# One DRAM sum for the layer-1 experts' results, with weights copied early, paired w_down loads and deeper prefetch

## The chip, the core and the metric

One core of a Trainium2 chip runs the whole program. The metric is the device time of one execution in microseconds. Lower is better.

## The reference, cut to what matters

Two transformer layers over 2048 tokens of 512 numbers. The part that the change touches:

```python
# layer 1 attention, keys: a small feature network with a bias fb1, applied to every head of k
#   feature = act(k_head @ fw1 + fb1) ...
# layer 1 feed-forward: 64 experts, 6 per token
topk_w, topk_ids = grouped_topk(sigmoid(x @ gate_w), bias)       # E = 64, K = 6, 8 groups, 4 kept
h   = silu(buf[e] @ w_gate[e]) * (buf[e] @ w_up[e])             # H = 512, F = 192
out = h @ w_down[e]                                             # F = 192 -> 512
y   = segment_sum(out[...] * topk_w, token)                     # each token: sum over its 6 experts
x   = layernorm(x + shared(x) + y)
```

## The kernel before

Matrix products are made in three passes (`mm3`, L64 to L68): both operands are split in a high and a low part, and high x high, high x low and low x high are added in PSUM. So every weight is copied to its high part by ACT and subtracted to its low part by DVE. Engines run programs of their own and meet at semaphores.

**Keys of layer 1** (`attention1_keys`). 16 tiles of 128 tokens. For each tile TensorE computes values (12 matmuls of 512 columns), then features: four groups of `mm3` with 128 rows of contraction and 256 columns (L66 to L68), each followed by one matmul that adds the bias from two rows (`ones2`, `fb_hl`, L1417), then sums (L1391, L1393) and the next keys.

**Shared expert and routing** (`experts1_shared`). Makes the tables `token_of` and `target_of` (which tokens an expert takes, and where its results go), and starts two DRAM sums: `sums[0]` with the residual, `sums[1]` with zeros (L1977, four DMAs of 1 MB out of a tile that DVE uses again at L2230), and spare rows of zeros.

**Routed experts** (`experts1_routed`). 64 experts of at most 96 tokens each. `three_stages` (L488) writes out each engine's order of work. Step g does on every engine, in this order: `ahead` for item g+3, `first` for g+1, `between` for g-1, `prepare` for g+1, `second` for g, `third` for g-1; the middle of the loop is a hardware loop unrolled U = 4 times. What an expert e passes through:

- SP loads (L2352, L2356): w_down of e when the low part of w_down of e-4 has been made, gate/up weights of e likewise. Four raw buffers of each.
- POOL `gather` (L2363 to L2372): copies the index (L2368), then an indirect DMA (L2371) brings 96 rows of 512 features and 64 expert shares into `xg`. It waits for the results of expert e-4, since `results` (L2472) still reads its scale from `xg`. Four buffers.
- PE `turn` (L2398), ACT and DVE parts (L2440, L2487), weight parts (L2447, L2482), gate/up products, silu (L2465), hidden (L2498), w_down parts (L2461, L2500), hidden turned (L2418), `down` with 96 rows of contraction twice.
- ACT `results` (L2472): scales by the share and writes `y`. Four buffers.
- POOL `add_results` (L2374 to L2383): copies the target (L2378), and an indirect DMA with add (L2382) adds 96 rows of 2 KB to `sums[e % 2]`. Two experts can hold the same token, so an add may only be issued when the last one to the same sum has landed: with two sums, that of e-2.

POOL's order in step g is gather(g+3), then add(g-1).

**Combine** (`combine1`). 8 groups of 256 rows: load both sums (L2520, L2521), add them on DVE (L2539), statistics (L93, L95), `rstd` on POOL (L100, L102), apply (L106), store (L2524).

Of the kernel before, what the change touches and what calls it, by code (L numbers as in the profile page):

```python
# [28 lines left out]
P = 128  # L29
# [458 lines left out]
def three_stages(eng, n, first, second, third, ahead=no_work, between=no_work, prepare=no_work, unroll=2):  # L488
# [5 lines left out]
    def step(g):  # L494

        for stage, item in ((ahead, g + 3), (first, g + 1), (between, g - 1), (prepare, g + 1), (second, g), (third, g - 1)):
            if 0 <= item < n:
                stage(item // unroll, item % unroll)


    rounds = (n - 4) // unroll
    for g in range(-3, unroll + 1):
        step(g)
    with eng.Fori(1, rounds) as i:
        for q in range(unroll):
            at = lambda stage, item: stage(i + item // unroll, item % unroll)
            at(ahead, q + 4)
# [694 lines left out]
def attention1_keys(k, xt, w):  # L1202
# [5 lines left out]
    with ExitStack() as ctx:  # L1208
# [7 lines left out]
        fb1 = sb("fb1", [2, FM])  # L1216
        part = sb("part", [2, 1])
        rest = sb("rest", [2, 1])
        fb_hi, fb_lo = sb("fb_hi", [2, FM], F32R), sb("fb_lo", [2, FM])
        fb_hl = sb("fb_hl", [2, 4, FM], F32R)  # L1220
        ones_f, ones2 = sb("ones_f", [2, P]), sb("ones2", [2, P], F32R)
# [63 lines left out]
        with nc.Block() as block:  # L1285
            @block.sync
            def _(sp):
# [5 lines left out]
                sp.dma_start(fb1[:, :], io["fb1"].partition_broadcast(2)).then_inc(s_fb, 16)  # L1293
# [3 lines left out]
                sp.wait_ge(s_zero, 12)  # L1297
# [11 lines left out]
            def _(pool):  # L1309
# [10 lines left out]
                pool.memset(rest[:, :], 1.0).then_inc(s_zero, 1)  # L1320
# [5 lines left out]
                pool.memset(part[0:1, :], 1.0).then_inc(s_zero, 1)  # L1326
                pool.memset(rest[0:1, :], 0.0).then_inc(s_zero, 1)
# [143 lines left out]
            def _(vec):  # L1471
# [4 lines left out]
                def feature_weights():  # L1476
                    vec.wait_ge(s_fw, 64)
                    vec.wait_ge(s_zero, 10)
# [408 lines left out]
def experts1_shared(k):  # L1887
# [6 lines left out]
    k.s_sums0, k.s_sums1 = k.sem("e1_first_sums_begun"), k.sem("e1_second_sums_begun")  # L1894
    k.w1_first = rt("w1_first", [P, KD, 2 * F1])
    k.s_w1_first = k.sem("e1_gate_up_loaded0")
    with ExitStack() as ctx:
# [66 lines left out]
        with nc.Block() as block:  # L1964
            @block.sync
            def _(sp):
# [17 lines left out]
                for c in range(NC):  # L1984
                    sp.wait_ge(s_res, TC * (c + 1))
                    sp.dma_start(k.sums[0][0:T, :].rearrange("(c j p) d -> c p j d", p=P, j=TC)[c],
                                 k.x[:, c * TC:(c + 1) * TC, :]).then_inc(k.s_sums0, 16)
# [183 lines left out]
            def _(vec):  # L2171
# [13 lines left out]
                def choose():  # L2185
# [42 lines left out]
                    vec.wait_ge(k.s_sums1, 16 * (NC + 2))  # L2228
# [82 lines left out]
def experts1_routed(k):  # L2311

    nc, bank, io = k.nc, k.bank, k.io
    with ExitStack() as ctx:
        U = 4
        two = lambda name, shape, dt=F32: [k.sb(f"e1_{name}{p}", shape, dt, ctx) for p in range(2)] * 2
        four = lambda name, shape, dt=F32: [k.sb(f"e1_{name}{p}", shape, dt, ctx) for p in range(U)]
        w1_raw = [k.w1_first] + [k.sb(f"e1_w1_raw{p}", [P, KD, 2 * F1], F32, ctx) for p in range(1, U)]
        w1_hi, w1_lo = two("w1_hi", [P, KD, 2 * F1], F32R), two("w1_lo", [P, KD, 2 * F1], F32R)
        w2_raw, w2_hi, w2_lo = four("w2_raw", [HF1, 2, D]), two("w2_hi", [HF1, 2, D], F32R), two("w2_lo", [HF1, 2, D], F32R)  # L2320
# [4 lines left out]
        si, hf = two("si", [CAP, F1]), two("hf", [CAP, F1])  # L2325
        ht_hi, ht_lo = two("ht_hi", [HF1, 2 * CAP], F32R), two("ht_lo", [HF1, 2 * CAP], F32R)
        y = four("y", [CAP, D])

        each = lambda name: [k.sem(f"e1_{name}{p}") for p in range(U)]
        sem = lambda n: k.sem("e1_" + n)  # L2330
        s_w = [k.s_w1_first] + [sem(f"gate_up_loaded{p}") for p in range(1, U)]
        s_v, s_g = each("down_loaded"), each("rows_gathered")
        s_y = [sem(f"results_added{a}") for a in range(2)]
# [8 lines left out]
        added = lambda h, p: 16 * (U // 2 * h + p // 2)  # L2342

        with nc.Block() as block:
            @block.sync
            def _(sp):
                def load(h, p):
# [14 lines left out]
            def _(pool):  # L2362
                def gather(h, p):  # L2363
# [10 lines left out]
                def add_results(h, p):  # L2374
                    e = U * h + p
                    if past(h, p, 2):
                        pool.wait_ge(s_y[p % 2], added(h, p))
# [4 lines left out]
                    pool.indirect_dma_start(k.sums[p % 2], bass.IndirectOffsetOnAxis(target[p][:, 0:1], 0), y[p][:, :], None,  # L2382
                                            compute_op=ALU.add).then_inc(s_y[p % 2], 16)  # L2383

                pool.wait_ge(k.s_sums0, 16 * NC)
                pool.wait_ge(k.s_sums1, 16 * (NC + 2))
                three_stages(pool, E1, nothing, nothing, add_results, ahead=gather, unroll=U)
                for a in range(2):
                    pool.wait_ge(s_y[a], 16 * E1 // 2)
# [231 lines left out]
```

## Time and profile before

| | us |
|---|---|
| median of 3 runs (1843.55 to 1856.09) | 1854.52 |
| the profiled execution | 1854.76 |
| its span in the trace | 1853.0 |

The profiled execution lies 0.2 us above the median, and 1.8 us of it lie outside of the span. Matmuls are pipelined and their ends modelled, so the distance from one start to the next tells more than a busy time. "q1 hardware_dynamic" are the DMAs that SP issues (weights among them), "q0 software_dynamic" those of POOL (gathers and adds).

### The profile page before, as it was taken

To read this page: it belongs to the slowest core of one execution; us is meant where nothing else is said; L and a number is where in the kernel's file an instruction comes from. 1 tells how busy PE (TensorE), PEld (TensorE's weight loads), DVE (VectorE), ACT (ScalarE), POOL (GpSimd) and SP (SyncE) were. 2 spreads that over 40 slices of the span, in tenths; PEclk is the share of its full clock that TensorE was granted. 3 is DMA by queue.
4 is the path that set the end of the run, shared out by engine and by line. 5 is a ranking of instruction groups with operands and counts; after the bars stand their busy time and mean duration, and the time that the engine had idled before them with its cause. 6 is when DMAs were issued, how large, how long until landed. Compare 5 with 4: busy or idle time off the path is not lost. (4 is left out here: it accounts for less than half of the span.)

```text
span 1853.0 us, 24141 instructions
## 1 busy us (share of the span) xinstructions
PE 1491.7 (81%) x8165; PEld 1249.9 (67%) x8166; DVE 1112.4 (60%) x1841; ACT 721.8 (39%) x1127; POOL 643.8 (35%) x738
## 2 busy tenths in 40 slices
PE   6999699997999996399997999688767767777760
PEld 5787476766999996388886888465555545555550
DVE  5787572345676774586535666366855555555556
ACT  3211230004666663144444444132135555555550
POOL 1455300003222221355331433115425554555553
PEclk8999899998999999699987999697768898888895
DMA  3000300007888884321000000231177888877767
GB/s 143 1 1 29 110 24 1 1 0 241 281 283 283 279 280 160 94 65 39 12 1 29 1 24 23 75 117 57 46 216 232 232 236 229 239 220 228 220 139 272
DMA packets 114934, 239.15 MB, mean 129 GB/s; under 512 B 13853, under 2 KB 48669, under 8 KB 114863
## 3 DMA queue, kind: packets, MB, share of 16 engines
q1 hardware_dynamic: 87647, 170.57, 27.8%
q0 software_dynamic: 18784, 51.39, 11.0%
q10 hardware_dynamic: 8432, 16.25, 2.3%
q8 instruction: 43, 0.70, 0.2%
q14 instruction: 28, 0.23, 0.0%
HBM read 187.45 MB, written 50.72 MB: 129 GB/s over the span
## 5 line engine op out<-in xcount | busy, mean ns | idle before, releaser
L66 PE MATMUL bank<-e_xt_hi,e_w_hi 128*128 128x256 f32 x496 | 142.9, 288 | 0.0
L2398 PE MATMUL bank<-ident,e_xg 96*128 96x96 f32 x256 | 40.1, 287 | 127.3 <-DMA e_xg<-rows,e_index 127.1
L68 PE MATMUL bank<-e_xt_hi,e_w_lo 128*128 128x256 f32 x496 | 140.2, 283 | 0.0
L67 PE MATMUL bank<-e_xt_lo,e_w_hi 128*128 128x256 f32 x496 | 140.1, 282 | 0.0
L2382 POOL DMA_INDIRECT sums<-e_y,e_target x64 | 117.9, 1842 | 58.5 <-POOL e_target L2378 22.1
L1047 POOL COPY e_index<-r_token_of 128x2 int32 (+1 forms) x31 | 7.9, 254 | 370.1 <-POOLq L602 203.4
L2398 PEld LDWEIGHTS bank<-ident,e_xg 96*128 96x128 f32 x256 | 28.1, 159 | 152.2 <-DMA e_xg<-rows,e_index 80.0
L1148 DVE TENSOR_TENSOR e_w_lo<-e_raw,e_w_hi 128x2048 fp32r<-128x2048 f32 x31 | 71.0, 2292 | 85.3 <-ACT e_w_hi L1105 70.8
L2487 DVE TENSOR_TENSOR e_xt_lo<-bank,e_xt_hi 128x384 fp32r<-128x384 f32 x64 | 35.6, 557 | 130.5 <-ACT e_xt_hi L2440 117.7
L66 PE MATMUL bank<-e_w_hi,e_xt_hi 128*96 128x384 f32 x256 | 106.4, 416 | 1.7 <-DVE e_w_lo L2482 1.7
L2482 DVE TENSOR_TENSOR e_w_lo<-e_w_raw,e_w_hi 128x1536 fp32r<-128x1536 f32 x48 | 84.4, 1759 | 35.5 <-ACT e_w_hi L2447 33.2
L68 PE MATMUL bank<-e_w_hi,e_xt_lo 128*96 128x384 f32 x256 | 102.3, 399 | 0.0
L67 PE MATMUL bank<-e_w_lo,e_xt_hi 128*96 128x384 f32 x256 | 102.0, 398 | 0.0
L67 PEld LDWEIGHTS bank<-e_xt_lo,e_w_hi 128*128 128x128 f32 x496 | 94.2, 190 | 0.0
L66 PEld LDWEIGHTS bank<-e_xt_hi,e_w_hi 128*128 128x128 f32 x496 | 94.1, 190 | 0.0
L68 PEld LDWEIGHTS bank<-e_xt_hi,e_w_lo 128*128 128x128 f32 x496 | 94.0, 189 | 0.0
L231 POOL TENSOR_TENSOR a_read<-a_read_n 128x256 f32<-128x256 f32 x64 | 50.2, 785 | 103.3 <-DVE a_read_n L452 103.3
L2440 ACT ACTIVATE e_xt_hi<-bank 128x384 fp32r<-128x384 f32 x64 | 31.2, 487 | 138.1 <-PE bank L2398 138.0
L1651 POOL TENSOR_TENSOR q_g_lo<-q_gf,q_g_hi 128x512 fp32r<-128x512 f32 x32 | 41.6, 1299 | 111.8 <-ACT q_g_hi L1765 111.8
L66 PE MATMUL bank<-s_xt_hi,s_w_hi 128*128 128x512 f32 (+1 forms) x192 | 78.6, 410 | 0.8 <-ACT s_scores L2148 0.8
L2371 POOL DMA_INDIRECT e_xg<-rows,e_index x64 | 61.1, 955 | 52.2 <-POOL e_index L2368 50.2
L1105 ACT ACTIVATE e_w_hi<-e_raw 128x2048 fp32r<-128x2048 f32 x31 | 59.4, 1916 | 49.2 <-DMA e_raw<-in_rw 29.4
(452 smaller groups left out, 5050.4 us busy)
## 6 DMA issues: line engine op xcount, KB each, us to landing
e_w_raw<-in_w_gate_up SPq DMA_DIRECT2D x48, 768.0 KB, 5.8
e_raw<-in_rw SPq DMA_DIRECT2D x62, 512.0 KB
e_w_raw<-in_w_down SPq DMA_DIRECT2D x64, 384.0 KB
e_raw<-in_rg SPq DMA_DIRECT2D x31, 512.0 KB
results<-e_y ACTq DMA_DIRECT2D x31, 512.0 KB, 5.7
r_w_first<-in_w_gate_up SPq DMA_DIRECT2D x16, 768.0 KB, 7.0
rows<-resid SPq DMA_DIRECT2D x8, 1024.0 KB, 4.3
resid<-in_x SPq DMA_DIRECT2D x4, 1024.0 KB, 11.3
```

Source lines behind the costliest of these rows:

```text
L66: pe.matmul(out, a_hi, b_hi, start=start, stop=False)
L67: pe.matmul(out, a_hi, b_lo, start=False, stop=False)
L68: return pe.matmul(out, a_lo, b_hi, start=False, stop=stop)
L231: pool.tensor_tensor(read_2[:, v % 2, :], read_n[:, v % 2, 0:256], read_n[:, v % 2, 256:512], ALU.add).then_inc(s_r2, 1)
L1105: act.activation(w_hi[p][:, 0:2 * W], raw[p][:, 0:2 * W], ACT.Copy).then_inc(s_whi, 1)
L1148: vec.tensor_tensor(w_lo[p][:, 0:2 * W], raw[p][:, 0:2 * W], w_hi[p][:, 0:2 * W], ALU.subtract).then_inc(s_wlo, 1)
L1651: pool.tensor_tensor(g_lo[:, c % 2, f], gf[:, u % 2, :], g_hi[:, c % 2, f].bitcast(F32), ALU.subtract).then_inc(s_glo, 1)
L2371: pool.indirect_dma_start(xg[p][:, :], None, k.rows1, bass.IndirectOffsetOnAxis(index[p][:, 0:1], 0)).then_inc(s_g[p], 16)
L2382: pool.indirect_dma_start(k.sums[p % 2], bass.IndirectOffsetOnAxis(target[p][:, 0:1], 0), y[p][:, :], None, compute_op=ALU.add).then_inc(s ...
L2398: mm = pe.transpose(bank[p % 2][:, b * CAP:(b + 1) * CAP], xg[p][:, b * P:(b + 1) * P], k.ident[0:CAP, 0:CAP])
L2482: vec.tensor_tensor(w1_lo[p][:, :, :], w1_raw[p][:, :, :], w1_hi[p][:, :, :], ALU.subtract).then_inc(s_wlo, 1)
L2487: vec.tensor_tensor(xt_lo[p][:, :], bank[p % 2][:, 0:KD * CAP], xt_hi[p][:, :], ALU.subtract).then_inc(s_tlo, 1)
```

## The change

1. **One sum.** `k.sums` is one DRAM tensor. add(e) waits for add(e-1) to land, not add(e-2). Four stores of 1 MB of zeros and one of spare rows go. `combine1` loads one sum, and DVE's add goes.
2. **Weights copied early.** DVE copies the expert's share out of `xg` into `weight` (96 x 1) right after `turned_lo`; gather(e) now waits for the copy of e-4 (`s_wt`), not for its results.
3. **Paired w_down loads.** w_down of two experts (3 x 128 rows) comes in one DMA of 128 partitions x 6 KB per two experts, not two of 96 x 4 KB. An even expert's parts are made of two blocks (1024 numbers per partition), an odd one's of one (512). The hidden tile is padded with zeros to 2 x 128 columns, so that `down` contracts 128 rows twice; each expert's 192 rows lie in blocks (0, 1) or (1, 2).
4. **Deeper prefetch.** U = 8, eight raw gate/up buffers and four raw pairs; `lead=6` on SP: loads run six experts ahead. All other engines keep `lead=3`, and gathers, targets and `y` keep four buffers (NX).
5. **Keys.** The bias operands `fb1`, `part`, `rest`, `ones_f`, `ones2`, `fb_hl` of `attention1_keys` have 128 partitions instead of 2, all but the first two rows zero in effect (`rest`, `part`), so the bias matmul contracts 128 rows. One more memset and one more wait on POOL.

```diff
-        for stage, item in ((ahead, g + 3), (first, g + 1), ...
+        for stage, item in ((ahead, g + lead), (first, g + 1), ...
@@ attention1_keys
-        fb1 = sb("fb1", [2, FM])
+        fb1 = sb("fb1", [P, FM])
...
-        ones_f, ones2 = sb("ones_f", [2, P]), sb("ones2", [2, P], F32R)
+        ones_f, ones2 = sb("ones_f", [P, P]), sb("ones2", [P, P], F32R)
@@ experts1_shared, SP
                 sp.wait_ge(s_zeros, 1)
-                for c in range(NC):
-                    sp.dma_start(k.sums[1][0:T, :].rearrange("(c j p) d -> c p j d", p=P, j=TC)[c],
-                                 zeros.unsqueeze(1).to_broadcast([P, TC, D])).then_inc(k.s_sums1, 16)
-                sp.dma_start(k.sums[0][T:T + CAP, :], zeros[0:CAP]).then_inc(k.s_sums1, 16)
-                sp.dma_start(k.sums[1][T:T + CAP, :], zeros[0:CAP]).then_inc(k.s_sums1, 16)
+                sp.dma_start(k.sums[T:T + CAP, :], zeros[0:CAP]).then_inc(k.s_spare, 16)
@@ experts1_routed, SP
-                    if past(h, p, U):
-                        sp.wait_ge(s_vlo, e - U + 1)
-                    sp.dma_start(w2_raw[p][:, :, :].rearrange("p f n -> p (f n)"),
-                                 io["w_down"][bass.ds(e, 1)].rearrange("e p n -> p (e n)")).then_inc(s_v[p], 16)
-                three_stages(sp, E1, nothing, nothing, nothing, ahead=load, unroll=U)
+                    if p % 2 == 0:
+                        if past(h, p, U):
+                            sp.wait_ge(s_vlo, e - U + 2)
+                        sp.dma_start(w2_raw[p][:, :, :].rearrange("p f n -> p (f n)"),
+                                     io["w_down"][bass.ds(U // 2 * h + p // 2, 1)].rearrange("q p n -> p (q n)")).then_inc(s_v[p], 16)
+                three_stages(sp, E1, nothing, nothing, nothing, ahead=load, unroll=U, lead=6)
@@ POOL
                 def gather(h, p):
-                    if past(h, p, U):
-                        pool.wait_ge(s_g[p], 16 * h)
-                        pool.wait_ge(s_ysb, e - U + 1)
+                    if past(h, p, NX):
+                        pool.wait_ge(s_g[p], gathered(h, p) - 16)
+                        pool.wait_ge(s_wt, e - NX + 1)
...
                 def add_results(h, p):
-                    if past(h, p, 2):
-                        pool.wait_ge(s_y[p % 2], added(h, p))
+                    if past(h, p, 1):
+                        pool.wait_ge(s_y, 16 * e)
...
-                    pool.indirect_dma_start(k.sums[p % 2], ...
+                    pool.indirect_dma_start(k.sums, ...
@@ PE, ACT, DVE
-                        mm = mm3(pe, bank[6 + p % 2][0:CAP, :], ht_hi[p][:, c], ht_lo[p][:, c], w2_hi[p][:, f, :], w2_lo[p][:, f, :],
+                        mm = mm3(pe, bank[6 + p % 2][0:CAP, :], ht_hi[p][:, c], ht_lo[p][:, c], w2_hi[p][:, p % 2 + f, :], w2_lo[p][:, p % 2 + f, :],
...
-                    if past(h, p, U):
-                        act.wait_ge(s_y[p % 2], added(h, p) - 16)
+                    if past(h, p, NX):
+                        act.wait_ge(s_y, 16 * (e - NX + 1))
+                    act.wait_ge(s_wt, e + 1)
...
+                    if past(h, p, NX):
+                        vec.wait_ge(s_ysb, e - NX + 1)
+                    vec.tensor_copy(weight[p][:, :], xg[p][:, bass.ds(D + e, 1)]).then_inc(s_wt, 1)
@@ combine1
-                    sp.dma_start(k.x[:, c * NL:(c + 1) * NL, :], tiles(k.sums[0][0:T, :])[c]).then_inc(s_a[c], 16)
-                    sp.dma_start(other[:, c * NL:(c + 1) * NL, :], tiles(k.sums[1][0:T, :])[c]).then_inc(s_b[c], 16)
+                    sp.dma_start(k.x[:, c * NL:(c + 1) * NL, :], tiles(k.sums[0:T, :])[c]).then_inc(s_a[c], 16)
...
-                    vec.tensor_tensor(k.x[:, t, :], k.x[:, t, :], other[:, t, :], ALU.add).then_inc(s_sum, 1)
```

## Rows read from the trace of the kernel before

**Rows 1.** The page's first line.
```profile
span 1853.0 us, 24141 instructions
```
**Rows 2.** Windows: stretch, us, each engine busy (instructions), TensorE clock, DMA share, GB/s.
```profile
786.00:966.00 180.00, 177.49 (x1036) 151.47 (x1034) 111.97 (x160) 77.97 (x148) 82.27 (x72) 0.93 0.10 30
1352.00:1380.00 28.00, 14.81 (x68) 11.72 (x68) 12.88 (x16) 12.84 (x18) 7.54 (x11) 0.65 0.86 274
1380.00:1802.00 422.00, 303.11 (x1468) 241.86 (x1468) 243.15 (x305) 239.59 (x366) 227.13 (x245) 0.86 0.78 222
1813.00:1853.00 40.00, 0.00 (x0) 0.00 (x0) 29.54 (x56) 0.00 (x0) 16.68 (x16) 0.50 0.84 315
...
799.00:813.00 14.00, 14.00 (x86) 11.90 (x85) 12.70 (x20) 6.84 (x14) 8.36 (x8) 1.00 0.18 53
```
**Rows 3.** Tile `e_target`: the adds, minimum/median/maximum ns, first and last start.
```profile
L2382 POOL DMA_INDIRECT sums<-e_y,e_target x64: 1422/1830/3022, 1380.3 to 1801.9; - x64
```
**Rows 4.** Timeline around one turn of the loop's chain: start, us, what, idle before.
```profile
1560.50 0.68 ACT L2472 ACTIVATE e_y<-bank,e_xg 96x512 f32<-96x512 f32 x1 [1.38 <-PE bank L68]
...
1562.39 0.95 POOL L2371 DMA_INDIRECT e_xg<-rows,e_index  x1 [0.80 <-POOL e_index L2368]
...
1569.56 0.55 PE L2398 MATMUL bank<-ident,e_xg 96*128 96x96 f32 x4 [1.50 <-DMA e_xg<-rows,e_index]
...
1573.89 0.68 ACT L2472 ACTIVATE e_y<-bank,e_xg 96x512 f32<-96x512 f32 x1 [0.50 <-PE bank L68]
```
**Rows 5.** Tile `e_xg` in 1400:1780: gathers, from issue to landing.
```profile
DMA to landing us min/median/max: 4.1/4.9/7.4
```
**Rows 6.** Timeline of TensorE in the keys stage, features of one tile.
```profile
909.44 0.28 PE L67 MATMUL bank<-a_fw_lo,k_k_hi 128*128 128x256 f32 x1
909.56 0.28 PE L68 MATMUL bank<-a_fw_hi,k_k_lo 128*128 128x256 f32 x1
909.77 0.38 PE L1417 MATMUL bank<-k_fb_hl,k_ones 2*128 2x256 f32 x1
910.08 0.39 PE L66 MATMUL bank<-a_fw_hi,k_k_hi 128*128 128x256 f32 x1
910.30 0.28 PE L67 MATMUL bank<-a_fw_lo,k_k_hi 128*128 128x256 f32 x1
```
**Rows 7.** Groups of TensorE in 786:970: the bias matmul.
```profile
L1417 PE MATMUL bank<-k_fb_hl,k_ones 2*128 2x256 f32 x64 | 24.4, 381 | 0.0
```
**Rows 8.** Timeline of POOL: adds and target copies.
```profile
1511.55 1.84 POOL L2382 DMA_INDIRECT sums<-e_y,e_target  x1 [0.85 <-ACT e_y L2472]
...
1571.06 0.20 POOL L2378 COPY e_target<-r_target_of 96x1 int32 x1
...
1572.12 1.45 POOL L2382 DMA_INDIRECT sums<-e_y,e_target  x1 [0.86 <-POOL e_target L2378]
...
1788.47 1.84 POOL L2382 DMA_INDIRECT sums<-e_y,e_target  x1 [0.85 <-ACT e_y L2472]
...
1793.05 0.18 POOL L2378 COPY e_target<-r_target_of 96x1 int32<-96x1 int32 x1 [0.24 <-DMA sums<-e_y,e_target]
```
**Rows 9.** DMA queues in 1512.6:1516.7, 1516.7:1519, 1574.1:1576.1, 1576.1:1579.5, 1405:1780: packets, MB, share of 16 engines.
```profile
q1 hardware_dynamic: 225, 1.09, 86.7%
...
q0 software_dynamic: 175, 0.42, 72.9%
...
q0 software_dynamic: 118, 0.20, 79.5%
...
q1 hardware_dynamic: 205, 0.96, 85.7%
...
q1 hardware_dynamic: 13854, 63.83, 51.4%
```
**Rows 10.** Timeline of DVE in the combine: first additions, statistics and apply.
```profile
1818.06 1.22 DVE L2539 TENSOR_TENSOR resid<-resid,c_other 128x1024 f32<-128x1024 f32 x1 [19.34 <-DMA c_other<-sums]
...
1821.76 1.22 DVE L2539 TENSOR_TENSOR resid<-resid,c_other 128x1024 f32<-128x1024 f32 x1 [0.74 <-DMA c_other<-sums]
...
1824.64 0.97 DVE L106 TENSOR_SCALAR resid<-resid,mv,rstd 128x512 f32<-128x512 f32 x2
1825.53 1.22 DVE L2539 TENSOR_TENSOR resid<-resid,c_other 128x1024 f32<-128x1024 f32 x1
```

More of the change, by code:

```diff
@@ L485, in no_work, with three_stages @@
     pass
-def three_stages(eng, n, first, second, third, ahead=no_work, between=no_work, prepare=no_work, unroll=2):
+def three_stages(eng, n, first, second, third, ahead=no_work, between=no_work, prepare=no_work, unroll=2, lead=3):
     def step(g):
-        for stage, item in ((ahead, g + 3), (first, g + 1), (between, g - 1), (prepare, g + 1), (second, g), (third, g - 1)):
+        for stage, item in ((ahead, g + lead), (first, g + 1), (between, g - 1), (prepare, g + 1), (second, g), (third, g - 1)):
             if 0 <= item < n:
                 stage(item // unroll, item % unroll)
-    rounds = (n - 4) // unroll
-    for g in range(-3, unroll + 1):
+    rounds = (n - lead - 1) // unroll
+    for g in range(-lead, unroll + 1):
         step(g)
@@ L2324, in experts1_routed @@
         xt_hi, xt_lo = two("xt_hi", [P, KD * CAP], F32R), two("xt_lo", [P, KD * CAP], F32R)
-        si, hf = two("si", [CAP, F1]), two("hf", [CAP, F1])
-        ht_hi, ht_lo = two("ht_hi", [HF1, 2 * CAP], F32R), two("ht_lo", [HF1, 2 * CAP], F32R)
+        weight = four("weight", [CAP, 1])
+        si, hf = two("si", [CAP, F1]), two("hf", [CAP, 2 * P])
+        own = lambda p: slice(p % 2 * (2 * P - F1), p % 2 * (2 * P - F1) + F1)
+        other = lambda p: slice(F1, 2 * P) if p % 2 == 0 else slice(0, 2 * P - F1)
+        ht_hi, ht_lo = two("ht_hi", [P, 2 * CAP], F32R), two("ht_lo", [P, 2 * CAP], F32R)
         y = four("y", [CAP, D])
-        each = lambda name: [k.sem(f"e1_{name}{p}") for p in range(U)]
         sem = lambda n: k.sem("e1_" + n)
         s_w = [k.s_w1_first] + [sem(f"gate_up_loaded{p}") for p in range(1, U)]
-        s_v, s_g = each("down_loaded"), each("rows_gathered")
-        s_y = [sem(f"results_added{a}") for a in range(2)]
+        s_v = [a for a in [k.sem(f"e1_down_loaded{q}") for q in range(U // 2)] for _ in range(2)]
+        s_g = [k.sem(f"e1_rows_gathered{p}") for p in range(NX)] * (U // NX)
+        s_zero, s_wt = sem("hidden_zeroed"), sem("weights_kept")
+        gathered = lambda h, p: 16 * (U // NX * h + p // NX + 1)
+        s_y = sem("results_added")
         s_ix, s_go, s_to = sem("index"), sem("index_seen"), sem("target")
@@ L2381, in add_results @@
                     pool.sem_inc(s_go, 1)
[L2382 to L2386, printed above, removed]
+                    pool.indirect_dma_start(k.sums, bass.IndirectOffsetOnAxis(target[p][:, 0:1], 0), y[p][:, :], None,
+                                            compute_op=ALU.add).then_inc(s_y, 16)
+                pool.wait_ge(k.s_sums, 16 * NC)
+                pool.wait_ge(k.s_spare, 16)
                 three_stages(pool, E1, nothing, nothing, add_results, ahead=gather, unroll=U)
-                for a in range(2):
-                    pool.wait_ge(s_y[a], 16 * E1 // 2)
+                pool.wait_ge(s_y, 16 * E1)
             @block.tensor
@@ L2393, in turn @@
                 def turn(h, p):
[L2394 removed]
+                    pe.wait_ge(s_g[p], gathered(h, p))
                     if past(h, p, 2):
@@ L2453, in hidden_hi @@
                         act.wait_ge(s_dn, e - 1)
-                    act.activation(ht_hi[p][:, :], bank[4 + p % 2][0:HF1, 0:2 * CAP], ACT.Copy).then_inc(s_hh, 1)
+                    act.activation(ht_hi[p][:, :], bank[4 + p % 2][:, 0:2 * CAP], ACT.Copy).then_inc(s_hh, 1)
                 def silu(h, p):
@@ L2510, in combine1 @@
     with ExitStack() as ctx:
-        other = k.sb("c1_other", [P, NT, D], F32, ctx)
-        s_a, s_b = ([k.sem(f"c1_{n}_loaded{c}") for c in range(NG)] for n in ("first", "second"))
-        s_sum = k.sem("c1_summed")
+        s_a = [k.sem(f"c1_sums_loaded{c}") for c in range(NG)]
         s_stat, s_var, s_rstd, s_ln, s_st = (k.sem("c1_" + n) for n in ("stats", "var", "rstd", "normed", "stored"))
@@ L2562, in two_layers @@
         k.rows1 = nc.dram_tensor("rows1", (T, D + E1), F32, kind="Internal").ap()
-        k.sums = [nc.dram_tensor(f"sums{a}", (T + CAP, D), F32, kind="Internal").ap() for a in range(2)]
+        k.sums = nc.dram_tensor("sums", (T + CAP, D), F32, kind="Internal").ap()
         setup(k)
```

65 lines of the change are left out of this document (34 added, 31 removed).

## The prediction

> **What bounds the kernel now.** I read the windows by stage first, then the stretches that the change touches. The profiled execution took 1854.8 us, 0.2 over the median, so the sum is made against 1854.8 [rows 1].
>
> In the keys stage TensorE is busy for 177.5 of 180 us: it alone sets the pace there, at a granted clock of 0.93 of full speed [rows 2]. Inside the features the full-height matmuls of 256 columns start 0.12 us apart, but around a bias matmul of two rows the spacing is 0.21 before it, 0.31 after its start, and 0.22 after the next start. One group of four takes 909.44 to 910.30, 0.86 us [rows 6].
>
> In the routed loop no engine is full: of 422 us TensorE is busy 303, DVE 243, ACT 240, POOL 227, and the DMA engines have a share of 0.78 [rows 2]. The 64 adds run from 1380.3 to 1801.9, so an expert takes 421.6 / 63 = 6.69 us [rows 3]. One turn of what holds it: results written at 1560.50, the gather that they release is issued at 1562.39, TensorE turns its rows at 1569.56, having waited for that DMA, and 4.3 us later, at 1573.89, results are written again [rows 4]. That is two steps in 13.4 us. The gather needs 4.1 to 7.4 us, 4.9 in the middle [rows 5]. So the loop is bound by the gather's latency, since `results` still reads `xg`. The steps themselves take 4.3 us.
>
> The combine, 1813 to 1853, is DVE's: after a first wait it repeats add, statistics, apply in 1825.53 - 1821.76 = 3.77 us [rows 2, 10].
>
> **The change part by part.**
>
> *Keys.* With 128 rows the bias matmul has the shape of its neighbours, which start 0.12 us apart, so a group of four should take 4 x 0.12 = 0.48 and not 0.86 us: 0.38 x 64 groups [rows 7] = 24.4 us less, all on the engine that sets the pace. The clock's mean of 0.93 means (1 - 0.93) x 180 = 12.6 us lost to half-speed stretches [rows 2]. They come while TensorE is never idle, so I suspect the sparse features, and put a third of it down as won: 4 us (bounds 0 and 12.6). DVE becomes the next limit in the first tiles: 12.7 of 14 us busy [rows 2] is 0.91 of a tile that is to shrink by 14%. For some six tiles that costs back about 0.5 us each, 3 us at most; I take 1. Sum: -28 (bounds -18 and -36). The wider memsets, the DMA of `fb1` to 128 partitions and one more POOL wait lie beside the loading of the stage and are costed at nothing; uncovered, they are below 1 us together.
>
> The Trainium skill (TensorE: Matmul & The Clock Gate, section LDWEIGHTS) says that loading 32 rows takes the same time as loading 128, as only columns count. By that alone the height of the bias operand would be worth nothing and the sum 28 us higher; the row speaks against it, as the neighbours with the same columns keep 0.12 us and this one does not [rows 6].
>
> *Combine.* Eight additions of 1.22 us go, 7 of them in rounds of DVE that start right behind one another and the first in front: 8 x 1.17 (the starts overlap by 0.05) = 9.4 us [rows 10]. Half of the loads go, so DVE starts on 0.5 MB instead of 1 MB, at 315 GB/s and more [rows 2] some 1.2 us earlier, and the 0.74 us wait for the second pair goes too, less what of it the shorter first round uncovers. Sum: -10.9 (bounds -9 and -12). Late next is still DVE, 2.6 us a group.
>
> *The stores of zeros.* Some 4.6 MB less written while TensorE and DVE set the pace of routing, and DVE never waited for them: 0.
>
> *The gather.* It no longer waits for the results of e-4 but for a copy made a step and more earlier. In POOL's order it stands behind add(g-2), so it leaves when that add has been issued. From there: add 1.8, index copy and issue some 2.0, gather 4.9 to 7.4, step 4.3, results to add 1.1 = 14 to 17 us for three steps: 4.7 to 5.5 us each. The gather's latency stops being the bound. DMA needs 0.78 x 6.69 = 5.2 us of all engines per expert [rows 2, 3], unchanged in bytes. ACT and DVE get about 0.3 us shorter (a quarter less of w_down on average) and DVE a copy of one column longer; neither was the bound.
>
> *The single sum.* This is what is late next. add(e) now goes out only when add(e-1) has landed. The period is: issue to release, then the target copy 0.20, then 0.86 to the issue [rows 8]. Queued behind this wait on POOL is the next gather, and behind that the whole loop. How long is issue to release? Low end: the add of 1788.47 freed the copy at 1793.05 after 4.58 us, when no weights were loaded any more [rows 8]; period 4.58 + 0.2 + 0.86 = 5.6 us. In mid-loop the add of 1572.12 had all its packets done by 1576.1, after which queue q0 has none [rows 8, 9]. High end: the add of 1511.55 had no packet moved until 1516.7, while q1 moved 1.09 MB of weights, and ended before 1519, 7.4 us after its issue [rows 8, 9]; with 0.6 to the release (4.58 against the 4.0 of the add of 1572.12) and 1.06 to the next issue the period is 9.1. Weights hold 51% of the DMA engines' time [rows 9], and the deeper prefetch bundles them: SP waits once per two experts for w_down's low part and then issues a pair and two gate/up loads, 2.3 MB. One of two adds should fall into such a bundle: (5.6 + 9.1) / 2 = 7.35. Against it, a gather now leaves some 4 us before the add and not 2, so the two no longer share the queue. I take 7.0 us (bounds 5.6 and 9.1). The last seven adds see no weights, since these run eight ahead: 5.6. Sum: 56 x 7.0 + 7 x 5.6 = 431 against 421.6, +9.6 us. The start, 1352 to 1380, is bound by gathers under a full queue and stays.
>
> Together: 1854.8 - 28 - 10.9 + 0 + 9.6 = 1825.5; I say 1825.
>
> **The rivals.**
>
> *Adds land fast.* If the adds fall mostly between the bundles, or get their turn among the weights, the period is 5.6 to 6.2. With 5.9: 56 x 5.9 + 39 = 370, -52 us, and 1854.8 - 28 - 10.9 - 52 = 1764; the floor, all at 5.6, is 1747. For it: the mid-loop add that took 4.0 us. Against it: the add of 1511.55, and that DMA would then be busy 5.2 of 5.9 us, with ever fewer gaps.
>
> The Trainium skill (DMA: Bandwidth & Descriptors, section Anatomy of one DMA) gives for a DMA of this path 2.0 us plus bytes / 436e3, an estimate of 2.5 us for 197 KB. By that page the chain of adds would not bind at all and this rival would win; the rows show 4.0 at the least.
>
> *The chain of adds costs more than all else gives (the other side).* Place: POOL's wait before L2378. Price: the keys and the combine give 38.9 us, so the kernel gets no faster if 56 x P + 39 = 460.5, P = 7.5 us; it is 1% slower from P = 7.9 on. With P = 8.0: 487, +66, 1882 us. For it: two adds of three would have to meet a bundle like that of 1511.55, and 2.3 MB at 274 GB/s [rows 2] last 8.4 us, more than one period. Against it: today's adds meet weights too, half of the time, and the loop holds 6.69.
>
> *The bias matmul's gap stays.* If it comes from something other than its two rows (its place, its bank), the keys give nothing: 1825 + 28 = 1853. Against it: the same shape without the gap stands beside it.
>
> **How the numbers follow.** Forecast (P from 6.5 to 7.5, keys as said): 1797 to 1853, chance 0.50. Fast adds: 0.22. Slow adds (P over 7.5): 0.18. Gap stays: 0.10. The range leaves out the faster half of the fast adds and the slower half of the slow ones: 1775 to 1872. A change of 1%, 18.5 us, is about what a measurement of this kernel can tell from none. Faster by over 1% (below 1836): 0.22 + 0.38 of the forecast's 0.50 = 0.60. Slower by over 1% (above 1873): half of the slow adds and a little of the last rival, 0.12. Same: 0.28. The predicted time is the forecast's own.
>
> **What would show it.** In the profile after: L1417 with starts 0.12 us apart from its neighbours, the keys stage some 150 us long and its clock closer to 1.00; in the loop TensorE's wait for the gather small or gone, and POOL's target copy waiting for the DMA of `sums` in nearly every step, at a period near 7; in the combine rounds of 2.6 us. The prediction is wrong if the adds' period is off (each 0.3 us is 17 us), if TensorE in the keys runs into ACT's or DVE's wait and gives only half, or if the loads bundled eight deep slow the gathers beyond their new slack.

## The result, and the profile after

The kernel after takes 1879.66 us (median of 4 runs, 1874.77 to 1885.87) against 1853.68 us for the kernel before: a ratio of 1.0153 with the interval 1.0103 to 1.0202: **slower by about 26 us, 1.5%**, which is small but clear of the noise. The forecast was 1825 us, with a range from 1775 to 1872. Below, P is the time of an expert in the routed loop: the last add's start less the first's, divided by 63.

The page's first line, after:
```profile
span 1876.2 us, 23909 instructions
```
Windows by stage of the kernel after (columns as in [rows 2]): keys, routed loop, combine.
```profile
799.00:939.00 140.00, 138.05 (x989) 129.67 (x988) 101.90 (x143) 71.50 (x142) 79.13 (x69) 0.98 0.11 30
...
1346.00:1838.00 492.00, 314.90 (x1482) 255.84 (x1480) 233.58 (x370) 228.99 (x370) 218.76 (x245) 0.81 0.65 190
1838.00:1876.00 38.00, 0.00 (x0) 0.00 (x0) 19.63 (x48) 0.00 (x0) 10.79 (x17) 0.50 0.65 226
```
One window of the kernel before, for the same 989 matmuls of the keys:
```profile
799.00:968.00 169.00, 169.00 (x989) 144.63 (x987) 102.25 (x143) 74.18 (x142) 78.77 (x69) 0.93 0.08 24
```
The adds after, by their tile (to set beside [rows 3]):
```profile
L2390 POOL DMA_INDIRECT sums<-e_y,e_target x64: 1423/1454/3024, 1346.0 to 1837.5; - x64
```
These rows split the 23.2 us by which the span grew. The first add starts 34.3 us earlier (1346.0 against 1380.3). From first to last add are 491.5 us and not 421.6: +69.9. From the last add to the end are 38.7 us and not 51.1: -12.4. The sum is +23.2. **Everything outside the loop gained what it was meant to and a little more; the loop lost more than all of it.** P went from 6.69 to 491.5 / 63 = 7.80 us, and the loop's DMA share fell from 0.78 to 0.65: nothing there is full.

*The loop.* Waits of the kernel after in 1346:1838 (engine, what waits, for whom: us in total, times, longest):
```profile
POOL e_target L2386 <- DMA sums<-e_y,e_target: 170.7, 59, 6.2
...
PE bank L2405 <- DMA e_xg<-rows,e_index: 165.9, 34, 7.1
```
POOL waits in nearly every step for the add before. TensorE's wait for the gather has not gone either: in 1352:1800 it is 158.7 us, where it was 127.1 before. The timeline of POOL shows why, in one full turn of two experts:
```profile
1542.23 1.46 POOL L2390 DMA_INDIRECT sums<-e_y,e_target  x1 [0.86 <-POOL e_target L2386]
1543.21 0.68 POOL L2376 COPY e_index<-r_token_of 96x1 int32 x1
1544.69 0.96 POOL L2379 DMA_INDIRECT e_xg<-rows,e_index  x1 [0.80 <-POOL e_index L2376]
1546.64 1.14 POOL L2386 COPY e_target<-r_target_of 96x1 int32 x1 [0.98 <-DMA sums<-e_y,e_target]
1548.62 1.76 POOL L2390 DMA_INDIRECT sums<-e_y,e_target  x1 [0.85 <-POOL e_target L2386]
1549.90 0.68 POOL L2376 COPY e_index<-r_token_of 96x1 int32 x1
1551.38 0.96 POOL L2379 DMA_INDIRECT e_xg<-rows,e_index  x1 [0.80 <-POOL e_index L2376]
1557.43 0.18 POOL L2386 COPY e_target<-r_target_of 96x1 int32 x1 [5.09 <-DMA sums<-e_y,e_target]
1558.46 1.45 POOL L2390 DMA_INDIRECT sums<-e_y,e_target  x1 [0.85 <-POOL e_target L2386]
```
The add of 1542.23 frees the next target copy after 4.4 us, the add of 1548.62 only after 8.8. The intervals are 6.39 and 9.84 us, in turn. What comes between is SP's bundle of three loads, issued as soon as VectorE has made the low part of w_down, 0.6 us behind the start of the second add's issue:
```profile
1548.37 0.68 DVE L2513 TENSOR_TENSOR e_w_lo<-e_w_raw,e_w_hi 128x512 fp32r<-128x512 f32 x1
...
1549.22 0.33 SPq L2361 DMA_DIRECT2D e_w_raw<-in_w_down  x1
...
1549.75 0.92 SPq L2356 DMA_DIRECT2D e_w_raw<-in_w_gate_up  x2
```
And the DMA queues, in 1544.2:1546.2 (the first add's packets), 1549.2:1554 (weights only, the second add has none), and 1554:1557 (both):
```profile
q0 software_dynamic: 112, 0.20, 79.9%
...
q1 hardware_dynamic: 211, 1.20, 75.9%
...
q1 hardware_dynamic: 138, 0.75, 63.0%
q0 software_dynamic: 129, 0.28, 42.1%
```
The second add's first packet moves 5.46 us after the start of its issue, its last at 8.05 us; without weights beside it the first add has 2.03 and 3.92 us. The pattern repeats every two experts: VectorE ends the w_down subtraction, which frees SP, at the point of the step where the next add goes out. The add was not ready ahead of the loads, though: its issue took POOL 1.76 us, to 1550.38, and the loads were issued from 1549.22 to 1550.67. Of the first 56 adds 25 land within 5 us and 31 later, and the mean interval behind them is 6.12 and 9.54 us; (25 x 6.12 + 31 x 9.54) / 56 = 8.01. The last 7 intervals, without weights, are 6.10 on average. The gather stands right behind the add in POOL's order and in queue q0, so behind a late add it lands late too (tile `e_xg` in 1400:1780):
```profile
DMA to landing us min/median/max: 5.8/7.7/8.9
```
This line knows the landing of 24 of the gathers there only, the ones behind the adds at SP's bundles. By their packets most of the others end about 3 us after their issue, and the mean of all is 5.1 us (5.4 in the kernel before). The line of [rows 5] likewise rests on 14 gathers of 55.


*The keys.* Timeline of TensorE in the kernel after, one group of four:
```profile
922.59 0.29 PE L66 MATMUL bank<-a_fw_hi,k_k_hi 128*128 128x256 f32 x1
...
922.94 0.28 PE L1419 MATMUL bank<-k_fb_hl,k_ones 128*128 128x256 f32 x1
923.06 0.28 PE L66 MATMUL bank<-a_fw_hi,k_k_hi 128*128 128x256 f32 x1
```
923.06 - 922.59 = 0.47 us where [rows 6] had 0.86. The stage's granted clock is 0.98 where it was 0.93.

*The combine.* DVE's rounds there (statistics, aggregate, apply):
```profile
1857.97 0.97 DVE L106 TENSOR_SCALAR resid<-resid,mv,rstd 128x512 f32<-128x512 f32 x2
1858.86 0.69 DVE L93 BATCH_NORM_STATS2 stats<-resid 128x6 f32<-128x512 f32 x1
...
1861.36 0.69 DVE L93 BATCH_NORM_STATS2 stats<-resid 128x6 f32<-128x512 f32 x1
```
A round is 1861.36 - 1858.86 = 2.50 us, against 3.77 in [rows 10].

### The profile page after: what moved, and what is told of

It is laid out like the page before. It is cut to its first block and busy times, and to the rows that moved or that the text cites. A ratio compares the mean times of both kernels' runs of the same rounds, so it can differ in the third digit from the quotient of the medians.

```text
span 1876.2 us, 23909 instructions
## 1 busy us (share of the span) xinstructions
PE 1468.7 (78%) x8165; PEld 1245.8 (66%) x8166; DVE 1089.8 (58%) x1897; ACT 705.7 (38%) x1127; POOL 629.2 (34%) x741
## 5 line engine op out<-in xcount | busy, mean ns | idle before, releaser
L2405 PEld LDWEIGHTS bank<-ident,e_xg 96*128 96x128 f32 x256 | 32.0, 171 | 197.7 <-DMA e_xg<-rows,e_index 115.0
L2390 POOL DMA_INDIRECT sums<-e_y,e_target x64 | 109.3, 1708 | 63.7 <-POOL e_target L2386 50.1
L2492 DVE TENSOR_TENSOR e_w_lo<-e_w_raw,e_w_hi 128x1536 fp32r<-128x1536 f32 x56 | 98.5, 1760 | 39.4 <-ACT e_w_hi L2456 38.6
L66 PE MATMUL bank<-e_w_hi,e_xt_hi 128*96 128x384 f32 x256 | 110.8, 433 | 0.2 <-DVE e_w_lo L2492 0.2
L2386 POOL COPY e_target<-r_target_of 96x1 int32 (+1 forms) x64 | 32.7, 512 | 170.8 <-DMA sums<-e_y,e_target 170.7
L2379 POOL DMA_INDIRECT e_xg<-rows,e_index x64 | 69.3, 1082 | 51.8 <-POOL e_index L2376 51.8
L2456 ACT ACTIVATE e_w_hi<-e_w_raw 128x1536 fp32r<-128x1536 f32 x56 | 83.2, 1486 | 0.0
```

The costliest lines, as they stand in the source:

```text
L66: pe.matmul(out, a_hi, b_hi, start=start, stop=False)
L2379: pool.indirect_dma_start(xg[p][:, :], None, k.rows1, bass.IndirectOffsetOnAxis(index[p][:, 0:1], 0)).then_inc(s_g[p], 16)
L2390: pool.indirect_dma_start(k.sums, bass.IndirectOffsetOnAxis(target[p][:, 0:1], 0), y[p][:, :], None, compute_op=ALU.add).then_inc(s_y, 16)
L2405: mm = pe.transpose(bank[p % 2][:, b * CAP:(b + 1) * CAP], xg[p][:, b * P:(b + 1) * P], k.ident[0:CAP, 0:CAP])
L2456: act.activation(w1_hi[p][:, :, :], w1_raw[p][:, :, :], ACT.Copy).then_inc(s_whi, 1)
L2492: vec.tensor_tensor(w1_lo[p][:, :, :], w1_raw[p][:, :, :], w1_hi[p][:, :, :], ALU.subtract).then_inc(s_wlo, 1)
```

## The experiments

Theory T1 (**bundle**): one sum makes a chain, issue, landing, target copy, issue, and the chain is long because every second add waits behind a bundle of weights. Theory T2 (**chain alone**): the chain takes over 7.3 us under any loads. Theory T3 (**held copy**): VectorE draws out POOL's copy and issue within the chain. Medians were measured beside the kernel before on the same chip; since its own median moves between 1852.8 and 1856.2 from group to group, ratios count. P, landing and gap are of one profiled execution each, which lay up to 6.4 us off its median (e13), so differences of P of 0.1 us tell nothing. The runs of e6 and e8 lie further apart than others (1853 to 1869, 1851 to 1868). Landing is the time from the start of an add's issue to the end of its last packet, and gap the time from there to the next issue, both as means of the first 56 adds.

| kernel | sums | weight copies | w_down loads | median us | ratio to before | P us | landing | gap |
|---|---|---|---|---|---|---|---|---|
| before | 2 | late | single | 1853.7 | 1 | 6.69 | 5.9 | 1.1 |
| after | 1 | early | pair | 1879.7 | 1.015 | 7.80 | 6.0 | 2.0 |
| e3 keys only | 2 | late | single | 1828.5 | 0.985 | 6.75 | 5.7 | 1.3 |
| e6 keys, one sum | 1 | late | single | 1866.4 | 1.004 | 7.49 | 5.8 | 1.9 |
| e7 keys, early | 2 | early | single | 1779.4 | 0.961 | 5.89 | 6.2 | - |
| e8 keys, early, one sum | 1 | early | single | 1865.1 | 1.003 | 7.60 | 5.9 | 1.9 |
| e1 two sums | 2 | early | pair | 1774.6 | 0.955 | 6.02 | 6.4 | - |
| e9 two sums, spread | 2 | early | pair at odd | 1759.7 | 0.949 | 5.71 | 5.9 | - |
| e11 e9, copy first | 2 | early | pair at odd | 1762.2 | 0.948 | 5.78 | 5.9 | - |
| e2 spread | 1 | early | pair at odd | 1843.3 | 0.994 | 7.34 | 5.7 | 1.8 |
| e5 copy first | 1 | early | pair | 1844.6 | 0.995 | 7.27 | 6.1 | 1.4 |
| e10 both | 1 | early | pair at odd | 1832.4 | 0.985 | 7.06 | 5.8 | 1.5 |
| e4 light loads | 1 | early | hardly any | 1780.5 | 0.959 | 6.22 | 4.2 | 2.1 |
| e12 light, copy first | 1 | early | hardly any | 1757.1 | 0.943 | 5.88 | 4.2 | 1.7 |
| e13 small subtraction | 1 | early | pair | 1842.0 | 0.994 | 7.32 | 5.8 | 1.7 |
| e14 one input | 1 | early | pair | 1835.7 | 0.989 | 7.11 | 5.6 | 1.7 |

**e1, the sum taken back.**
```diff
-                    if past(h, p, 1):
-                        pool.wait_ge(s_y, 16 * e)
+                    if past(h, p, 2):
+                        pool.wait_ge(s_y[p % 2], added(h, p))
...
-                    pool.indirect_dma_start(k.sums, ...
+                    pool.indirect_dma_start(k.sums[p % 2], ...
```
(the stores of zeros and the combine are those of the kernel before.)

> The kernel after, with two sums again (even experts add into one, odd experts into the other; both are zeroed, and the combine adds the two). Early weight copies, paired w_down loads and the new keys stay. If it is the chain through one sum that made the loop 7.80 us per expert, the loop falls to 5.5 to 6.2 us (the gather or the gate/up work bounds it, as 6.69 us did with later weight copies), 63 x 1.6 to 2.3 = 100 to 145 us less, and the combine takes its 12 us back: 1745 to 1790. If the paired loads themselves hold up the gathers, it gives back less: 6.7 us per expert and about 1820. The rival that neither is so (the loop is bound by loads at 200 GB/s) says 7.8 and about 1890.

Measured: 1774.61 us, ratio 0.9546 (0.9515 to 0.9576). The adds of this kernel:
```profile
L2395 POOL DMA_INDIRECT sums<-e_y,e_target x64: 1423/1455/2944, 1346.4 to 1725.5; - x64
```
379.1 / 63 = 6.02 us. **The one sum alone costs 105 us of time and turns a gain of 4.5% into a loss of 1.5%.** The adds land no sooner here (6.4 us on average, as the bundle hits them too); they only no longer follow one another.

**e2, the bundle spread.**
```diff
-                    if p % 2 == 0:
+                    if p % 2 == 1:
                         if past(h, p, U):
-                            sp.wait_ge(s_vlo, e - U + 2)
+                            sp.wait_ge(s_vlo, e - U + 1)
```


> The kernel after, but the paired w_down load is issued at the odd expert and not together with two gate/up loads, so that no single issue round puts more than the pair and one gate/up load on the queues. Bundle theory (every second add lands 8.0 us after its issue and not 3.9, since 1.5 to 2.2 MB of weights stand ahead of it): the late add gains 1 to 2 us, the period falls from 7.80 to about 7.2, 1830 to 1850. Chain theory (issue, landing, copy, issue take their time whatever the loads, and the bytes per two experts are the same): 7.7 to 7.9 us and 1870 to 1885.

Measured: 1843.29, ratio 0.9936 (0.9910 to 0.9962), P = 7.34. The late adds land after 7.1 us on average and not 7.65, the early ones unchanged at 3.9, and 31 of 56 are late, as in the kernel after. This is near T1's 7.2 and below T2's 7.7 to 7.9, but the bundle's form is worth 0.46 us and no more: the bytes still come. What refutes T2 is e4 below.

**e3, the keys alone** (the kernel before with `attention1_keys` of the kernel after).

> The kernel before with the keys of the kernel after alone (bias matmul moved). The first add came 34.3 us earlier in the kernel after, of which the keys show 29. If all 34 are the keys' own: 1819; if 5 belong to the early weight copies or the zeroing of one sum: about 1824; if the forecast's 24 were the matmuls alone and the clock gave nothing: 1830. The loop should stay at 6.69 us per expert.

Measured: 1828.51, ratio 0.9852 (0.9830 to 0.9873), 27.5 us less; P as before. Its windows:
```profile
799.00:940.00 141.00, 136.59 (x982) 128.41 (x980) 101.25 (x142) 71.47 (x141) 80.47 (x71) 0.98 0.10 28
1350.00:1774.00 424.00, 303.17 (x1468) 243.26 (x1468) 242.49 (x304) 239.84 (x366) 228.13 (x244) 0.86 0.78 220
```
The forecast had 28. From the first to the last bias matmul it is 143.5 us against 173.2. The start of the first add is no fine measure: in kernels whose code up to the loop is that of the kernel after it lay between 1340.4 and 1349.4.

**e4, the weights taken out.**
```diff
-                        sp.dma_start(w1_raw[p][:, :, :].rearrange(...), io["w_gate_up"][bass.ds(e, 1)]...)
+                        if past(h, p, U):
+                            sp.dma_start(w1_raw[p][:, 0, 0:16], io["w_gate_up"][0][:, 0:16]).then_inc(s_w[p], 16)
```
(and the same for w_down.)

> The kernel after, but from expert 8 on each weight load brings 16 columns of a block only (it leaves out nearly all of loading the weights of experts 8 to 63, which compute with stale ones). One sum stays. Bundle theory: no add meets weights, all land about 3.9 us after issue, and the period is that plus the copy and the issue, 5.6 to 6.6 us: 63 x 1.2 to 2.2 less than 1880, 1740 to 1800. Chain theory: adds are bound by their own 128 descriptors, the copies and VectorE beside them, and the period stays above 7.3: over 1845. The last seven adds of the kernel after, without weights beside them, took 5.3 and 6.6 us in turn, which speaks for about 6.

Measured: 1780.49, P = 6.22, landing 4.2 us. (An add is 112 packets of q0, as above, and not 128.) POOL's timeline there:
```profile
1541.10 1.45 POOL L2396 DMA_INDIRECT sums<-e_y,e_target  x1 [0.86 <-POOL e_target L2392]
...
1545.44 0.18 POOL L2392 COPY e_target<-r_target_of 96x1 int32 x1 [0.91 <-DMA sums<-e_y,e_target]
1546.47 2.12 POOL L2396 DMA_INDIRECT sums<-e_y,e_target  x1 [0.86 <-POOL e_target L2392]
...
1551.52 0.18 POOL L2392 COPY e_target<-r_target_of 96x1 int32 x1 [0.32 <-DMA sums<-e_y,e_target]
```
The alternation is gone: 53 of 56 adds land within 5 us. **7.80 - 6.22 = 1.58 us of P are the weights' doing**, and T2, which asked for over 7.3 under any loads, is refuted. But 6.22 us with hardly any loads is still more than the 6.02 of e1, which moves them all.

**e5, the target copy ahead of the wait.**
```diff
-                    if past(h, p, 1):
-                        pool.wait_ge(s_y, 16 * e)
                     pool.tensor_copy(target[p][:, :], k.target_of[:, bass.ds(e, 1)]).then_inc(s_to, 1)
                     pool.wait_ge(s_to, e + 1)
+                    if past(h, p, 1):
+                        pool.wait_ge(s_y, 16 * e)
```


> The kernel after, but the copy of an add's target indices is made before the wait for the add before it, so that only the add's own issue stands behind that wait. The copy took 0.6 us alone and up to 1.4 us beside VectorE's two-input operations, once in each period. Held-copy theory: 1.0 to 1.4 us less per expert, 7.80 to 6.4 to 6.8, 1790 to 1815. Plain theory (the copy is worth its 0.6 us): 7.2, about 1840. If the landing of the late add is what its weights dictate (it then waits for the same end of the load bundle), the copy gives nothing: 7.7 and 1875.

Measured: 1844.57, ratio 0.9947 (0.9929 to 0.9966), P = 7.27. The plain value: the gap falls from 2.03 to 1.36 us, by 0.67, and the landing gives 0.10 of it back. The stronger form of T3 (1.0 to 1.4 us) is refuted.

**e6, one sum on the old base** (the kernel before with the new keys, one sum, and the combine of the kernel after).

> The kernel before with the new keys and one sum, but the old weight copies and single loads: the one-sum part of the change on the base that its forecast was read from. In the kernel after, one sum against two (the run with two sums) cost 7.80 - 6.02 = 1.78 us per expert; with the old loads, keys alone gave 1828.5 at 6.75 us. If the cost of one sum needs the paired loads (bundle), the loop goes to 6.9 to 7.2 us here: 1828.5 + 63 x 0.15 to 0.45 - 12 = 1826 to 1845. If one sum has its price under any loads (chain), it is 7.6 to 7.9: 1870 to 1890.

Measured: 1866.44, ratio 1.0038 (1.0006 to 1.0070), P = 7.49. It is the base from which P was forecast, and the value lies between the two theories, nearer to the chain's 7.6: one sum costs 0.74 us per expert here, 1.78 with early copies and pairs. The chain sets 7.5 to 7.8 either way; what differs is how fast the loop would run without it.

**e7, the early weight copies without pairs.**
```diff
-                        pool.wait_ge(s_ysb, e - U + 1)
+                        pool.wait_ge(s_wt, e - U + 1)
...
-                                   scale=xg[p][:, bass.ds(D + e, 1)]).then_inc(s_ysb, 1)
+                                   scale=weight[p][:, 0:1]).then_inc(s_ysb, 1)
```


> The kernel before with the new keys and the early weight copies; two sums, single w_down loads. Beside the run with two sums (early copies and paired loads, 6.02 us per expert, 1774.6) and the keys alone (6.75, 1828.5) it tells which of the two brought the 54 us. Early copies alone: about 6.0 and 1775. Paired loads alone: 6.7 and 1825.

Measured: 1779.36, ratio 0.9612 (0.9584 to 0.9640), P = 5.89. **The early copies alone bring 0.86 us per expert, 49 us.** The pairs and the deeper prefetch, which no run takes apart, bring little beside that: P is no lower in e1 (6.02), while its median is 4.7 us lower and its ratio 0.0066, some 12 us.

**e8, the same with one sum.**

> New keys, early weight copies and one sum, but w_down by single loads: the kernel after without its paired loads. One sum costs 0.74 us per expert with the old copies and single loads (6.75 to 7.49), 1.78 with early copies and paired loads (6.02 to 7.80), of which 0.46 to 0.53 went when the pair was spread or the target copy taken out of the chain. If the chain of adds alone sets the period, the early copies give nothing here and it stays at 7.4 to 7.5: 1840 to 1860, and the pairs cost the rest, some 0.3 us. If pairs cost nothing: 7.8 and 1878.

Measured: 1865.05, ratio 1.0026 (0.9996 to 1.0056), P = 7.60. The early copies, worth 49 us with two sums, are worth nothing behind one (e6: 7.49). Against the kernel after the pairs, with the deeper prefetch, cost 0.20 us per expert. Nor does it take the bundle to make adds late: with single loads 34 of 56 land after more than 5 us in e6 and 40 in e8, but after 6.8 and 6.6 us on average, not 7.65. So the weights' bytes are the cause, and their bundling is the smaller part of it; T1 holds in this weaker form.

**e9, e11, the best version.** e9 is e1 with the edit of e2; e11 also has the edit of e5.

> Two sums, new keys, early weight copies, and the paired w_down load issued at the odd expert. With one sum the same move gave 7.80 to 7.34 us per expert. If the loop with two sums is still bound by adds and gathers that stand behind a bundle, it falls from 6.02 to 5.6 or 5.8: 1750 to 1762. If two sums already hide the late add, nothing: 1770 to 1780. Slower, above 1785, if the pair issued later is late for its expert.

> Two sums, new keys, early copies, the paired load at the odd expert (5.71 us per expert, 1759.7) and the target copy ahead of the wait for the add before last. With two sums POOL hardly waits for an add any more, so the copy should give nothing: 1755 to 1765. If POOL's wait for the add still holds some experts, 1750.

Measured: e9 1759.67, ratio 0.9487 (0.9460 to 0.9514), P = 5.71; e11 1762.24, P = 5.78, no gain. Spreading the pair helps with two sums as well, 0.31 us per expert and 15 us. e9 is 5.1% faster than the kernel before and 6.4% faster than the kernel after, with two sums.

**e10, both cures on one sum.**

> One sum with both cures: the paired load at the odd expert, and the target copy ahead of the wait. Alone they gave 0.46 and 0.53 us per expert. If they are two separate terms of one chain: 7.80 - 0.99 = 6.8 us, 1815. If both only move the add out of the same bundle: 7.25, 1840.

Measured: 1832.39, ratio 0.9846 (0.9804 to 0.9887), P = 7.06, between both expectations: the cures overlap by 0.25 of 0.99 us.

**e12, light loads and the copy first.**

> The light-load kernel (one sum; it leaves out nearly all of loading the weights of experts 8 to 63) with the target copy ahead of the wait. There the add landed 4.2 us after its issue and the next was issued 2.1 us later, 6.22 together. If those 2.1 us are the copy (0.6 to 1.4) in the chain, the period falls to 5.0 to 5.5: 1705 to 1735. If it is then bound elsewhere (the gather, gate/up), it stays at 5.9 or more: 1760 to 1780.

Measured: 1757.14, P = 5.88; the copy gave 0.34 us, and the time lies just below the second expectation (5.9 and 1760), far from the first. Among its waits those of TensorE for the gather come first (85.6 us before weight loads, 79.1 before matmuls), and POOL's for the add is no longer among the largest; something other than the add holds part of the experts there, which I did not take apart.

**e13, e14, does VectorE hold POOL?** In the kernel after the target copy takes 0.89 us on average in the 30 cases where an operation of VectorE with both inputs in SBUF overlaps it and 0.18 (at most 0.19) in the 34 others, among them 7 that overlap one which reads an input from PSUM; the add's issue takes 2.02 us in 29 such cases against 1.45 in the 35 others.
```diff
# e13 (from expert 8 on)
-                    vec.tensor_tensor(w1_lo[p][:, :, :], w1_raw[p][:, :, :], w1_hi[p][:, :, :], ALU.subtract)
+                    vec.tensor_tensor(w1_lo[p][:, 0, 0:16], w1_raw[p][:, 0, 0:16], w1_hi[p][:, 0, 0:16], ALU.subtract)
# e14 (and the same for w2_lo)
-                    vec.tensor_tensor(w1_lo[p][:, :, :], w1_raw[p][:, :, :], w1_hi[p][:, :, :], ALU.subtract)
+                    vec.tensor_copy(w1_lo[p][:, :, :], w1_raw[p][:, :, :])
```


> The kernel after, but from expert 8 on VectorE subtracts only 16 columns of one block for the low part of the gate/up weights, and not 1536 (it leaves out the rest of that low part; 1.76 us of VectorE per expert go). If VectorE's two-input operations hold up POOL: the target copy falls from a mean of 0.52 us to 0.3 or less, the add's issue from 1.71 to below 1.6, and the period of 7.80 by 0.3 to 0.6 us: 1840 to 1860. If it is a coincidence: copies and issue as before, and the period falls at most by what the shorter prepare brings to a loop that is not bound by it, nothing: 1875 to 1880.

> The kernel after with both low parts of the weights made by a one-input copy of the full size and not by the subtraction (it leaves out the subtraction: the low part is the weight itself), so VectorE is as busy or nearly so, with one input read. If what holds POOL is a second input stream, POOL's target copy falls to 0.2 to 0.3 us on average and the period by 0.3 to 0.6 us, 1840 to 1860. If any long VectorE operation does it, copies stay near 0.5 and the time near 1875.

Measured: e13 1841.97, ratio 0.9937 (0.9914 to 0.9961), P = 7.32. POOL's copies in it, and under it in the kernel after (group lines of POOL: line, operation, count | busy us, mean ns | idle before):
```profile
L2386 POOL COPY e_target<-r_target_of 96x1 int32 (+1 forms) x63 | 13.7, 218 | 164.2 <-DMA sums<-e_y,e_target 164.1
```
```profile
L2386 POOL COPY e_target<-r_target_of 96x1 int32 (+1 forms) x63 | 32.6, 517 | 170.8 <-DMA sums<-e_y,e_target 170.7
```
The copy fell from 0.52 to 0.22 us and the add's issue from 1.71 to 1.53, although that subtraction ends none of the waits in the chain of adds; it is the cause of the long copies. These account for one half of the shorter period: the interval behind an early add fell from 6.12 to 5.56 us, that behind a late one stayed (9.48), and 28 adds are early and not 25. The last may come from the loads, which the shorter subtraction also frees sooner; no run tells. e14: 1835.73, ratio 0.9886 (0.9846 to 0.9927), P = 7.11, copy 0.30 us. It does not say that one input frees POOL: the one-input copy ran in 0.98 us and not 1.76, so it also has less to hold with, and it does hold, as VectorE's and POOL's timelines of e14 show:
```profile
1500.26 0.96 DVE L2492 CAST e_w_lo<-r_w_first 128x1536 fp32r<-128x1536 f32 x1 [0.71 <-ACT e_w_hi L2456]
```
```profile
1500.29 0.98 POOL L2386 COPY e_target<-r_target_of 96x1 int32 x1 [1.40 <-DMA sums<-e_y,e_target]
```
POOL's 0.18 us copy ends with VectorE's, at 1501.2. That the one started second waits for the other's end is what the Trainium skill says (SBUF — State Buffer, section Who interferes with whom), for an operation with two inputs there and for some fast copies; the trace agrees on both, with 0.89 against 0.18 us and with this row.

## Why the prediction was wrong, by its own steps

**The step that failed is the single sum's term**, "I take 7.0 us (bounds 5.6 and 9.1)", and in it the estimate, not the mechanism. Late next was the add, as said; POOL's target copy waits for it in 59 steps of 64, 170.7 us in all. But the mean of the first 56 was 8.01. Against 7.0 the pieces are:
- Share: not one add of two, 28, but 31 of 56 meet weights, 3 x 3.5 us = 10 us.
- The early interval was 6.12 and not 5.6, 25 x 0.52 = 13 us. The row behind 5.6, the add of 1788.47 [rows 8], was followed by an undisturbed target copy of 0.18 us; in mid-loop VectorE draws out every other one, and without that the early interval is 5.56 (e13).
- The late interval was 9.54 and not 9.1, 31 x 0.44 = 14 us. The bound "9.1" was the one hit I had looked at, and it was not the worst.
- The discount of 0.35 us, "the two no longer share the queue", 56 x 0.35 = 20 us, is the plain error. The gather does leave 3.9 us ahead of the next add, as said (1544.69 and 1548.62), but that saved nothing: no packet of a gather lies inside any of the 25 early adds, and they take the same 3.9 us for their packets as the 4.0 of the row. No run shows the term.
- The last seven: 6.10 and not 5.6, 3.5 us.

Together 60 us, which is the 491.5 against 431. The mean of the two bounds, 7.35, without the discount, would have been nearer, at 1845, and e2 to e14 show how firm the rest is: no one-sum version with its weights loaded came below 7.06.

The landing was not what changed: its mean is 5.9 us over the 56 adds of the kernel before and 6.0 in the kernel after. Two adds of mid-loop were read, one of 4.0 and one of 7.4 us; the mean of all 56 in the same trace, with the 0.6 us to the release and the 1.06 us to the next issue that the prediction itself took, gives 5.9 + 1.66 = 7.5 us, the breaking point of its own rival.

**The rival that came true** is the chain that costs more than all else gives: it named POOL's wait, the breaking point of 7.5 and 1882 us at P = 8.0. It had 0.18. Two arguments held it down. "Two adds of three would have to meet a bundle" took the early interval as 5.6; with 6.12 and 9.54 the 31 of 56 that there were make 8.0. "Today's adds meet weights too, half of the time, and the loop holds 6.69" was no argument at all: in the kernel before 41 of 56 adds land after more than 5 us, and with two sums an add may land late (6.4 us in e1) at no cost, since the next one doesn't wait for it.

**What 6.69 was compared with.** I set P against the 6.69 of the kernel before, and so called the term +9.6. The loop that the change gives up is the one with early copies: 5.89 (e7). "The gather's latency stops being the bound" and "4.7 to 5.5 us" were right in direction only: the size is 5.9, and with two sums TensorE still waits 78.9 us for the gather (e1). The true price of one sum is 1.78 us x 63 = 112 us, less 13 in the tail: 99 by the spans (1876.2 - 1777.5), 105 by the medians.

**Keys:** forecast -28, measured -27.5 by e3. The traces show -30: the pitch of 0.47 us for 0.86 is 25 of it, and the clock, 0.98 for 0.93, the other 5, net of the 2 us that TensorE now idles in 140 (4 put down). **Bias gap stays:** refuted; with the full height the gap is gone. The Trainium skill (TensorE: Matmul & The Clock Gate, section LDWEIGHTS) says that loading few rows takes the time of 128. The trace agrees for the load itself, 0.181 us with two rows and 0.187 to 0.192 with 128, and yet the matmuls around a two-row one are spaced wider; why is open. **Combine:** forecast -10.9, measured -12.4. **Start, zero stores:** no gain seen, as said. **Fast adds** (5.6 to 6.2 us): refuted where weights are loaded, and without them 6.22 just misses it. The landing of 3.9 to 4.2 us with no weights beside it stands against the 2.5 us that the fit of the Trainium skill (DMA: Bandwidth & Descriptors, section Anatomy of one DMA) gives as an estimate.

## What to carry to other kernels

A wait for a DMA's landing that is put between two DMAs of one loop turns a latency that nobody paid into the loop's period; price it as landing plus everything up to the next issue, taken under the loads that the loop really has, and against the loop that you would have without it. If accumulating DMAs must be ordered among themselves, two targets used in turn are worth far more (105 us here) than the work that their merging costs (13 us). Take the latency as the mean over all steps of the trace, not from one good and one bad case. And look at what is issued together: where a prefetch and the critical DMA are released at the same point of the step, they meet again and again (31 of 56 here); moving the prefetch by one expert gave back 0.46 us of 7.80.

## What the runs showed of the hardware

- An accumulating DMA of 96 x 2 KB has its last packet 3.9 us after the start of its issue with no weights beside it (mean of 25; 4.2 in e4), and 7.65 us (mean of 31) where up to 2.3 MB of loads go out beside it. The first packet alone then takes 4.7 us on average (5.5 in the turn shown) instead of 2.0: that its issue starts 0.6 us ahead of the loads' gave the add no precedence.
- VectorE's operations with both inputs in SBUF hold POOL's copies until they end, and draw out its DMA issues: a copy of 0.18 us became 0.89 on average, an issue of 1.45 us 2.02, and 0.30 of the 0.52 us mean went with one VectorE instruction per expert (e13); a one-input copy holds too (e14).
- Sixty-four matmuls of two rows among ones of 128 cost 0.39 us each (0.86 - 0.47), and something of the clock: the stage without them had a granted clock of 0.98, with them 0.93, though TensorE was busy for 169.00 us of 169 with them (and 138.05 of 140 without).
